# Attention and expert layer on one core: the normalised input goes through DRAM and VectorE turns it, where TensorE turned it before

## The reference, cut to what matters

```python
x_norm = (x - mean(x)) / sqrt(var(x) + 1e-5) * gamma + beta       # x: 4 batches x 2048 rows x 512
q, k, v = x_norm @ qkv[:, :512], x_norm @ qkv[:, 512:1024], x_norm @ qkv[:, 1024:]
attn = softmax(where(causal, q @ k.T / sqrt(512), -inf))          # per batch, 2048 x 2048
x = layernorm(x + (attn @ v @ o_proj + x))
h = silu(silu(x @ w1.T) @ w3.T) @ w2.T                             # then 2 of 8 experts' gates per row,
out = zeros.at[chosen expert].add(gate * h)                        # added into rows 0..7
x = layernorm(x + out)
```

## Time and profile before

| what | value |
| --- | --- |
| median of 3 runs | 1683.85 us (1682.76 to 1684.57) |
| profiled execution | 1682.32 us |
| its span, first to last instruction | 1680.3 us |
| busy: PE, DVE, ACT, POOL | 98%, 49%, 40%, 17% |
| PE idle in the span | 1680.3 - 1650.4 = 29.9 us |

### The profile page before, as it was taken

One profiled execution on the slowest core, in us unless ns is written; L12 is line 12 of the kernel. 1 busy time (PEld: TensorE's weight loads), 2 busy tenths in 40 slices (PEclk: granted clock), 3 DMA queues, 4 the chain that ended last, 5 costly groups with the idle time before them and its releaser, 6 DMA issues.

```text
span 1680.3 us, 23574 instructions
## 1 busy us (share of the span) xinstructions
PE 1650.4 (98%) x7923; PEld 1369.7 (82%) x7923; DVE 828.1 (49%) x2168; ACT 671.6 (40%) x1301; POOL 282.6 (17%) x491
## 2 busy tenths in 40 slices
PE   7999999999999999999999999999999999999998
PEld 5888888878888888788888888888878888888886
DVE  5454434454453445455343456443456556555563
ACT  5443333443342334343322445332344444444443
POOL 1120201111120111121110112010122212212121
PEclk9999999999999999999999999999999999999999
DMA  4111201121111011121101132111154223132200
GB/s 157 57 51 51 70 32 38 64 71 63 70 51 51 32 50 64 58 101 49 53 19 38 45 100 95 38 57 45 63 115 74 36 39 50 25 50 43 32 0 7
DMA packets 173764, 92.58 MB, mean 55 GB/s; under 512 B 137296, under 2 KB 137296, under 8 KB 173664
## 3 DMA queue, kind: packets, MB, share of 16 engines
q1 hardware_dynamic: 162768, 72.41, 15.8%
q10 hardware_dynamic: 10896, 18.90, 3.6%
HBM read 57.71 MB, written 33.57 MB: 54 GB/s over the span
## 4 chain that ended last, share of the span: by engine, by line
PE 79%; issue 13%; POOL 3%; ACT 3%; DVE 2%; DMA 1%; SPq 0%; ACTq 0%; POOLq 0%; DVEq 0%
PE psum L334 24%; PE psum L336 24%; PE psum L335 24%; PE psum L1221 3%; PE psum L1159 1%; POOL rstd L454 1%; PE psum L1326 1%; PE psum L1325 1%; PE psum L1318 1%; PE psum L1317 1%; ACT xin L580 1%; ACT tok L580 1%; POOL expo L529 1%; ACT affine L564 0%; DVE stats L823 0%
## 5 line engine op out<-in xcount | busy, mean ns | idle before, releaser
L334 PE MATMUL psum<-xt_hi,g_hi 128*128 128x512 f32 (+3 forms) x640 | 239.5, 374 | 0.4 <-DVE g_lo L849 0.4
L628 ACT ACTIVATE pt_hi<-psum 128x512 fp32r<-128x512 f32 (+3 forms) x160 | 84.8, 530 | 369.6 <-PE psum L1221 363.7
L336 PE MATMUL psum<-xt_lo,g_hi 128*128 128x512 f32 (+3 forms) x640 | 230.0, 359 | 0.0
L335 PE MATMUL psum<-xt_hi,g_lo 128*128 128x512 f32 (+3 forms) x640 | 229.2, 358 | 0.0
L334 PE MATMUL psum<-v_hi,pt_hi 128*128 128x512 f32 x544 | 222.8, 410 | 1.8 <-DVE pt_lo L859 1.4
L336 PE MATMUL psum<-v_lo,pt_hi 128*128 128x512 f32 x544 | 213.1, 392 | 0.0
L335 PE MATMUL psum<-v_hi,pt_lo 128*128 128x512 f32 x544 | 212.8, 391 | 0.0
L451 POOL TENSOR_TENSOR var_eps<-meanvar,eps 128x2 f32<-128x2 f32 (+1 forms) x97 | 19.3, 199 | 1048.8 <-DVE meanvar L827 1046.7
L864 DVE TENSOR_REDUCE rowmax<-psum 128x1 f32<-128x512 f32 (+3 forms) x160 | 97.5, 610 | 197.7 <-PE psum L336 197.2
L746 ACT ACTIVATE act_f<-psum 128x512 f32<-128x512 f32 x128 | 76.5, 598 | 210.0 <-PE psum L336 210.0
L529 POOL TENSOR_TENSOR expo<-euler,shifted 128x32 f32<-128x32 f32 x16 | 86.9, 5430 | 298.0 <-DVE shifted L1061 298.0
(11 more groups left out here) (145 smaller groups left out, 3401.7 us busy)
## 6 DMA issues: line engine op xcount, KB each, us to landing
xin<-in_x ACTq DMA_DIRECT2D x64, 256.0 KB, 2.8
tok<-in_x SPq DMA_DIRECT2D x64, 256.0 KB, 2.6
x_scratch<-tok SPq DMA_DIRECT2D x64, 256.0 KB, 2.0
out_dram<-tok SPq DMA_DIRECT2D x64, 256.0 KB, 2.0
x_in<-x_scratch SPq DMA_DIRECT2D x64, 256.0 KB, 4.2
xin<-in_w_t ACTq DMA_DIRECT2D x8, 256.0 KB, 2.8
w_sb<-in_w_t SPq DMA_DIRECT2D x1, 1024.0 KB, 5.2
raw<-in_wq_t SPq DMA_DIRECT2D x1, 768.0 KB, 6.1
```

Source lines behind the costliest of these rows:

```text
L334: pe.matmul(o, ws, ms, start=first, stop=False, skip_group_check=True)
L335: pe.matmul(o, w_lo, ms, start=False, stop=False, skip_group_check=True)
L336: return pe.matmul(o, ws, m_lo_, start=False, stop=last, skip_group_check=True)
L628: act.activation(pt_hi[:, n % 2, 0:w], psum[:, turn_bank(turn_use(t, c)), 0:w], ACT.Copy).then_inc(pt_hi_ready, 1)
```

## The change

The normalised input is stored to a DRAM scratch (`xn_scratch`) by SP and read back group by group into `xt_b`, with its 32x32 blocks already placed. DVE turns the inside of the blocks (`turn_x`, four instructions of 128x512 a group, into `xt_a`), ACT applies gamma and beta from SBUF (`affine_x`), and DVE rounds and subtracts as before. `xt_a` and `xt_b` lie in the memory of `xt_hi` and `xt_lo`. Only group 0 of the first batch is still turned by TensorE. The input is loaded by SP, one pair a DMA, one to three pairs further ahead. The loop now runs from tile 7 to tile 6 (`PEELED = 7`). `turn_probs(15, 0)` moves from tile 15 to the end of tile 14. In the opening TensorE first runs 14 products of the identity, the folds of the weights are interleaved otherwise, and three pairs of x are loaded early.

```diff
-        PEELED = 2
+        PEELED = 2 * GROUP - 1
+        WARMING = 14
...
+            def load_xq(b, g):
+                rows_of = xn_scratch[bass.ds(b * S + g * (GROUP * P), GROUP * P), :].rearrange("(t j) (c q i) -> q j c t i", j=LANES, q=QUADRANTS, i=LANES)
+                for c in range(DC):
+                    for q in range(QUADRANTS):
+                        sp.dma_start(xt_b[q * LANES:(q + 1) * LANES, c, columns(g)].rearrange("j (t i) -> j t i", i=LANES),
+                                     rows_of[q][:, c]).then_inc(xq_loaded[g % 2], DMA)
...
+                if t == TILES - 1 and not last:
+                    sp.wait_ge(scores_ready, b * CHUNKS + BEFORE[t] + 1)
+                    load_xq(b + 1, 0)
...
+                if normed:
+                    sp.wait_ge(xn_stored, stored(*normed))
+                    to_load = ahead(b, first_half(g) if k else second_half(g), last)
+                    if to_load:
+                        load_x(*to_load)
+                if k == GROUP - 1:
+                    if g + 2 < GROUPS:
+                        sp.wait_ge(scores_ready, b * CHUNKS + 1)
+                        load_xq(b, g + 2)
+                    elif g + 2 > GROUPS and not last:
+                        sp.wait_ge(scores_ready, b * CHUNKS + BEFORE[t] + 2)
+                        load_xq(b + 1, g + 2 - GROUPS)
...
+            def affine_x(b, g, c):
+                act.wait_ge(xq_turned, (b * GROUPS + g - 1) * DC + c + 1)
+                act.activation(xt_b[:, c, columns(g)], xt_a[:, c, columns(g)],
+                               ACT.Identity, bias=beta_sb[:, c:c + 1], scale=gamma_sb[:, c:c + 1]).then_inc(affine_ready, 1)
...
+            def turn_x(b, g, c):
+                dve.wait_ge(xq_loaded[g % 2], (2 * b + (g + 1) // 2) * DC * LOADS)
+                dve.transpose(xt_a[:, c, columns(g)], xt_b[:, c, columns(g)]).then_inc(xq_turned, 1)
...
+                if t == TILES - 2:
+                    split_probs(b, TILES - 1, 0)
                 if t == TILES - 1 and last:
                     split_wr()
+                if t == TILES - 2 and not last:
+                    for c in range(DC):
+                        turn_x(b + 1, 0, c)
+                    split_x(b + 1, 0, 0)
+                    split_x(b + 1, 0, 1)
+                    norm_x(*ahead(b, second_half(g), last))
+                if more and (k == 0 and g or t == 1 and not before):
+                    for c in range(DC):
+                        turn_x(b, g + 1, c)
...
-                if more and k == 0:
-                    turn_x(b, g + 1, 0)
...
                     if c + 1 < chunks(t):
                         turn_probs(b, t, c + 1)
-                    if more and k == 2 and c == chunks(t) - 1:
-                        turn_x(b, g + 1, 3)
...
+                    elif t == TILES - 2:
+                        turn_probs(b, TILES - 1, 0)
                     attend(b, t, c)
```

More of the change, by code:

```diff
@@ L346, in load_x1, with x_pair, pair_rows, stored @@
                                  rows_of[q]).then_inc(x1_loaded[slot], DMA)
+        def x_pair(n, first):
+            if first and n in EARLY:
+                return xt_a[:, n - 1, 2 * GROUP * P:4 * GROUP * P].rearrange("p (s d) -> p s d", s=2)
+            return xin[:]
+        def pair_rows(dram, b, pair):
+            return dram[bass.ds(b * S + 2 * pair * P, 2 * P), :].rearrange("(s p) d -> p s d", p=P)
+        def stored(b, pair):
+            return (b * PAIRS + pair - 1) * DMA
+        def second_half(g):
+            return 2 * (g + 2) + 1
+        def first_half(g):
+            return 2 * (g + 3)
+        def ahead(b, pair, last):
+            if pair < PAIRS:
+                return b, pair
+            return None if last else (b + 1, pair - PAIRS)
+        def columns(g):
+            return slice(GROUP * g * P, GROUP * (g + 1) * P)
         block = whole.enter_context(nc.Block())
@@ L476, in tile @@
                 pool.tensor_tensor(y, y, y, ALU.add).then_inc(res_doubled, 1)
[L477 to L480, removed]
+                if k == GROUP - 1 and ahead(b, first_half(g), last):
+                    norm_x(*ahead(b, first_half(g), last))
                 if t:
@@ L484, in tile @@
                     norm_behind(b - 1, TILES - 1)
[L485 to L490, removed]
+                if t == 0 and not before:
+                    norm_x(b, EARLY[2])
+                if k == 2 and ahead(b, second_half(g), last):
+                    norm_x(*ahead(b, second_half(g), last))
             def batch(b, last):
@@ L497, in batch @@
                         tile(b + 1, t)
-            for pair in range(FIRST_PAIRS):
+            for pair in range(FIRST_PAIRS - 1):
                 norm_x(0, pair)
@@ L828, in statistics, with norm_x @@
                 done.then_inc(requested, 1)
[L830 to L838, removed]
-                value = affine[:].rearrange("p (k n) -> p k n", k=2)
+            def norm_x(b, pair, first=False):
+                if first and pair in EARLY:
+                    dve.wait_ge(x_early_loaded[pair - EARLY[0]], DMA)
+                else:
+                    dve.wait_ge(x_loaded, (pair + 1) * DMA if first else (b * PAIRS + pair - 2) * DMA)
+                if not first or pair:
+                    dve.wait_ge(x_normed, b * PAIRS + pair)
+                y = x_pair(pair, first)
+                statistics(lambda s: y[:, s - 2, :], 2, 4, x_variance)
@@ L934, in tile @@
                     split_v(b, t + 1)
-                if t == TILES - 2 and not last:
-                    split_x(b + 1, 0, 1)
                 if t == TILES - 1 and not last:
@@ L951, in tile @@
                     split_probs(b, t, 3)
+                if t == TILES - 2:
+                    split_probs(b, TILES - 1, 0)
                 if t == TILES - 1 and last:
                     split_wr()
+                if t == TILES - 2 and not last:
+                    for c in range(DC):
+                        turn_x(b + 1, 0, c)
+                    split_x(b + 1, 0, 0)
+                    split_x(b + 1, 0, 1)
+                    norm_x(*ahead(b, second_half(g), last))
+                if more and (k == 0 and g or t == 1 and not before):
+                    for c in range(DC):
+                        turn_x(b, g + 1, c)
+                if more and k == 1:
+                    for c in range(2 if g else DC):
+                        split_x(b, g + 1, c)
                 if more and k == 2:
-                    split_x(b, g + 1, 3)
                     split_v(b, GROUP * (g + 1))
+                    if ahead(b, second_half(g), last):
+                        norm_x(*ahead(b, second_half(g), last))
                     split_g(b, g + 1)
@@ L959, in tile @@
                         split_v(b, GROUP * (g + 1) + j)
-                if more and k == 0:
-                    norm_x(b, 2 * (g + 1) + 1)
-                if t == TILES - 2 and not last:
-                    norm_x(b + 1, 1)
+                if t == 0 and not before:
+                    norm_x(b, EARLY[2], first=True)
                 from_tile = TILES - 1 - GROUP
@@ L978, in batch @@
                     row_bias(b + 1, 0)
-                    norm_x(b + 1, 2)
                     residual(b, TILES - 1)
+                    for c in range(DC):
+                        turn_x(b + 1, 1, c)
                     split_v(b + 1, 0)
```

269 lines of the change are left out of this document (146 added, 123 removed).

## The result

The changed kernel takes 1696.35 us (median of four runs, 1696.04 to 1697.59) against 1683.99 us, 12.4 us more; the ratio is 1.0076, with a 95% interval of 1.0058 to 1.0093. The forecast was slower, 1690 with a range of 1664 to 1702. The profiled execution is 14.1 us longer than that of before.

What follows compares the result with a forecast made beforehand. PE, busy 98% of the span, was taken as the bound. Terms -4.6 + 16.2 + 0.4 + 1.8 + 0 - 10.7 + 0.8 + 2.7 = +6.6 on 1682.3 gave 1688.9, stated as 1690 us; range 1664 to 1702.

Steps and rivals of the forecast that it cites:

- DVE's seven rows ahead of `residual(14)`: Four turns, two splits, statistics; with residual done 18.6 us after tile 14's last score chunk (S), PE waits 6.1 at attend(15, 0).
- VectorE's list is hidden: Rival, chance 0.20: DVE's added work makes PE wait less; 1650 us if all hidden, 1669 if only tile 15's wait remains.
- Boundary: Tile 14 to tile 2 of the next batch: +5.4 us each, three times, +16.2; bounds +3 and +8 each.
- the one from there to `attend(2)`: From the next batch's projection to attend(2): four units leave (-1.8), waits of 1.85 and 1.1 come, sum +1.1 us.
- The wait at `attend(1)`: PE in tile 1 waits 1.85 us because four affines stand ahead of pt_hi on ACT.
- Jump: Loop's end, moved from tile 2 to tile 7: the 2.39 us wait occurs wherever it stands, term 0.
- Clock: Behind PE's 6.1 us waits at the batch boundaries the clock may fall: 0.6 us each, +1.8 in all.
- Last batch: norm_behind(13) on ACT stands behind the copy of (15, 0), so the x_in load comes 2.7 us later: +2.7 us.
- Tiles 3 to 13: Tiles 6, 8 and 10: 24 units leave PE, -10.7 us; a split ahead of a difference in tile 10 adds +0.8.
- Tiles 3 to 5: Tile 4: two units and a 0.54 us wait leave, but ACT's affines delay tile 5's difference; 0, bounds -5.7 and +3.2.
- Opening: Start to first projection: -4.6 us, folds from 7.5 us, one new wait of about 1.0; bounds -6 and -3.

Runs made afterwards that it cites:

- Experiment 1: Changed kernel with DVE's four turns, two splits and input statistics moved earlier in tile 14, and ACT's two affines ahead of the copy for (15, 0): 1674.58 us.
- experiment 9: Changed kernel with the edits of Experiment 1 and experiment 2, old last-batch order, earlier fourth split, norm_behind of tile 2 behind tile 4's first copy: 1651.91 us.
- experiment 6: Kernel before, with only the loop's end moved to between tiles 6 and 7 (PEELED = 7): 1678.62 us.
- experiment 2: Changed kernel with ACT's four affines behind the copies of tiles 1, 5 and 9, and two of group 1's splits moved to tile 2 on DVE: 1681.83 us.
- experiment 3: Changed kernel with only two of group 1's four splits moved on DVE from the end of tile 1 into tile 2: 1690.5 us.
- experiment 5: Changed kernel with identity products on PE ahead of attend(15, 0) in batches 0 to 2: 1702.92 us with 48 products, 1693.40 us with 24.

## Why the prediction was right, and where its terms were off

**Direction and place: right.** The forecast rested on one place, DVE's seven rows ahead of `residual(14)`. They were forecast to end 18.6 us behind S, and PE's wait to be 6.1. Measured, they end 326.05 - 308.03 = 18.0 behind it, PE's idle time is 5.51 three times, and `attend(15, 0)` comes 3.4 later than before (forecast 3.9). Experiment 1 shows the cause: with the order alone changed, it goes. *VectorE's list is hidden*, the rival on the other side, failed at the point named for it, DVE not being done when PE arrived. It is what the kernel becomes with the rows in other places: 1651.9 us in experiment 9, near the 1650 of that rival.

**Boundary: the place right, the size short.** Forecast 5.4 and 0.6 for the clock. Counted from S, and with the 2.3 and 2.2 us that the jump took away at the first two (experiment 6) added again, the boundaries became 7.1, 6.6 and 7.7 us longer. Up to the first product of the next batch's projection the forecast was right: +5.1, +4.6 and +5.7, against 4.3 and 0.6. The step that failed is the one from there to `attend(2)`: +1.1 forecast, +2.0 measured three times. The wait at `attend(1)` is 1.80 as forecast (1.85), but that at `attend(2)` is 1.82, not 1.1. DVE's timeline ahead of it, with the second and the third of these rows from the four splits and the last `residual(1)`:

```profile
366.97 0.42 DVE L955 TENSOR_TENSOR pt_lo<-psum,pt_hi 128x256 fp32r<-128x256 f32 x1 [4.92 <-ACT pt_hi L713]
...
370.92 0.69 DVE L939 TENSOR_TENSOR xt_lo<-xt_b,xt_hi 128x512 fp32r<-128x512 f32 x1
...
371.99 1.56 DVE L939 TENSOR_TENSOR xt_lo<-xt_b,xt_hi 128x512 fp32r<-128x512 f32 x1
...
375.59 0.74 DVE L979 SCALAR_TENSOR_TENSOR tok<-psum,rinv,tok 128x512 f32<-128x512 f32 x1
```

DVE stands still for the copy behind the affines and then has work up to the residual. One of the four subtractions takes 1.56 us, at all three boundaries, where the forecast had 0.69 for each; these 0.87 us are more than the 0.7 by which the wait was too small. Why it is longer no run shows. Experiments 2 and 3 tell the two waits apart.

**Jump: wrong.** That the 2.39 us "occurs wherever the loop's end stands" failed. It is mostly hidden at tile 7 (0.24 us of idle time, the other not listed), and experiment 6 gained 5.1 us by this alone. This error, about 3.6 us with what tile 7 takes back, has the other sign than the rest and made the total look better than its terms: that 1690 came within 6.4 us of 1696.35 is in part luck.

**Clock: right in kind, wrong in place.** All three long waits were followed by the lower pace: 0.63 us for 0.39, at a granted clock of 0.50. The Trainium skill, page "TensorE: Matmul & The Clock Gate", section "Why this matters for your kernels", says of idle gaps between matmuls that they send the clock back; this trace agrees, with the numbers of the sentence before. Net it cost the boundaries 1.1 us by experiment 5 (forecast 1.8), because a later wait took up the loss. What the prediction lacks is that shorter waits may do it too: the lower pace stands behind the wait of 1.82 in tile 2 of batch 2 (683.47, +1.5) and in the last batch behind that of 2.10 at 1253.74 (+1.6). It also stands in the tail (+1.7), where the last eight matmuls took 3.62 us before and 5.31 after:

```profile
1671.74 3.62 PE L1379 MATMUL psum<-w_sb,acc_t 128*128 128x512 f32 x8
```

```profile
1684.35 5.31 PE L1479 MATMUL psum<-w_sb,acc_t 128*128 128x512 f32 x8
```

Ahead of these PE waits 1.45 and 0.73 us in both kernels, so no new wait explains the tail; its cause stays open. In experiment 5 the same eight took 3.62 with the 24 products and 5.32 with the 48. Together the three places are 4.8 us for which the forecast had no term.

**Last batch: right, and the clock on top.** The load is 2.6 us late (forecast 2.7); +4.5 was measured, and 1.6 of it is the lower pace behind the second wait.

**Tiles 3 to 13.** 24 units at 0.445 (-10.7) and the late difference of tile 10 (+0.8) gave -9.9. From tile 5 to tile 13 it was -9.1, of which the jump's rest at tile 7 takes +0.9: right. Tiles 3 to 5, forecast 0, cost 0.5 in each batch but the first, about 1.5 in all. The forecast had the wait in tile 5, but not one in tile 4:

```profile
413.90 0.47 PE L345 MATMUL psum<-v_hi,pt_hi 128*128 128x512 f32 x1 [1.06 <-DVE pt_lo L955]
...
423.87 0.47 PE L345 MATMUL psum<-v_hi,pt_hi 128*128 128x512 f32 x1 [0.69 <-DVE pt_lo L955]
```

Together they take more than the 1.4 that the two units and their wait leave. The second goes in experiment 2 and stays in experiment 3, so it comes from the affines. The first falls to 0.7 in experiment 2 and goes in experiment 9, so most of it comes from `norm_behind` of tile 2.

**Opening.** -3.5 at the first projection, not -4.6: there are two new waits on PE (0.63 for ACT's affine, 1.08 for a low part of the weights), where one of 1.0 was reckoned with, and the folds started at 8.32 instead of 7.5.

## What to carry to other kernels

When work moves from the bounding engine to one that is half idle, look for the one instruction there that the bounding engine waits for, and add up what the new order puts ahead of it; the share of busy time says nothing on that. The same instructions were 12 us slower than the original in one order and 32 us faster in another. About 5 of the 32 are no merit of the turn on VectorE: the place of the loop's end alone gives as much to the original (experiment 6). A wait that is made longer costs more than itself, if the engine's clock falls in it, but measure whether a later wait takes that up.

## What the runs showed that was not expected

- Waits of 1.8 us on PE were followed by the lower pace in some places and executions (683.47 in the changed kernel) and not in others (376.95, 992.64); waits of 5.5 us were followed by it each time, 15 of 15 in the five traces that have them.
- The 2.4 us at the loop's end were hidden nearly whole when the end came behind projections.
- An fp32 product of 128x128 on PE took 0.22 us, in two rows of 0.11, where a transposing one takes 0.11.
